# Gated cross-attention and quantised feed-forward, one core: the second stage's rounded rows are turned by transposing transfers instead of TensorE and VectorE

## What is computed

```python
def _quant_per_tensor(x):
    scale = jnp.maximum(jnp.max(jnp.abs(x)), MIN_RANGE) / QP
    return (_ste_round(x / scale), scale)

def _qlinear(x2d, w, b):
    xq, sx = _quant_per_tensor(x2d)
    wq, sw = _quant_per_tensor(w)
    out = jnp.matmul(xq, wq.T) + b[None, :]
    return out * (sw * sx)

h = _qlinear(x.reshape(-1, D), w1, b1)
h = jax.nn.gelu(h, approximate=False)
o = _qlinear(h, w2, b2)

x = x + jnp.tanh(g_xattn[0]) * _L0_xattn_ref(_layernorm(x), ctx, ctx, ...)
x = x + jnp.tanh(g_ffn[0]) * _L0_ffn_ref(_layernorm(x), w1, b1, w2, b2)
```

## Time and profile before

| | us |
|---|---|
| median of 3 runs | 451.65 (450.1 to 454.19) |
| the profiled execution | 451.68 |
| its span, first to last instruction | 449.8 |
| TensorE matmul busy | 411.2 (91%) |
| VectorE busy | 350.6 (78%) |
| ScalarE busy | 275.4 (61%) |
| GpSimd busy | 124.7 (28%) |

### The profile page before, as it was taken

How to read it: one execution, slowest core, us unless ns; L and a number is a source line. 1 busy time by engine, 2 the same in 40 slices (tenths; PEclk the granted TensorE clock), 3 DMA queues, 4 the chain that set the end, 5 groups by cost and what they waited for, 6 DMA issues and landing times.

```text
span 449.8 us, 6567 instructions
## 1 busy us (share of the span) xinstructions
PE 411.2 (91%) x2236; PEld 254.3 (57%) x2236; DVE 350.6 (78%) x666; ACT 275.4 (61%) x478; POOL 124.7 (28%) x169
## 2 busy tenths in 40 slices
PE   6879969999999878868499999999999999999996
PEld 5646858778777567753244444444464444444442
DVE  4887682999996737989998899889759787666762
ACT  2157253897887255838098689869969999560000
POOL 2364671887888140323910000000000000000000
PEclk9997787999999668999699999999999999999999
DMA  6999650293345012124256676400019999962222
GB/s 232 359 366 405 203 195 1 104 313 146 133 146 186 1 38 103 47 94 189 93 240 281 280 305 283 201 1 0 0 34 373 414 425 411 398 212 93 94 95 93
DMA packets 14637, 85.37 MB, mean 190 GB/s; under 512 B 1784, under 2 KB 2048, under 8 KB 5136
## 3 DMA queue, kind: packets, MB, share of 16 engines
q1 hardware_dynamic: 14464, 84.74, 49.6%
q10 hardware_dynamic: 144, 0.26, 0.2%
HBM read 55.64 MB, written 29.36 MB: 189 GB/s over the span
## 4 chain that ended last, share of the span: by engine, by line
PE 78%; DVE 12%; issue 3%; SPq 2%; ACT 2%; DMA 1%; POOL 1%; DVEq 0%; ACTq 0%; POOLq 0%
PE PS L1187 24%; PE PS L1155 23%; PE PS L1070 6%; PE PS L1053 6%; PE PS L1005 6%; PE PS L1051 4%; PE PS L1042 3%; PE PS L1021 3%; DVE ring L853 2%; PE PS L1117 2%; DVE hmax L681 1%; DVE X L717 1%; DMA X<-in_x 1%; SPq L280 1%; PE PS L1013 1%
## 5 line engine op out<-in xcount | busy, mean ns | idle before, releaser
L548 ACT ACTIVATE ring<-PS,bias,sc 128x512 f32<-128x512 f32 x128 | 97.2, 782 | 36.5 <-PE PS L1155 24.6
L1155 PE MATMUL PS<-mid,w1q 128*128 128x512 bf16 x512 | 113.5, 382 | 0.9 <-DVE mid L869 0.9
L1187 PE MATMUL PS<-w2q,w1q 128*128 128x512 bf16 x512 | 110.8, 379 | 1.3 <-DVE w1q L936 0.9
L1187 PEld LDWEIGHTS PS<-w2q,w1q 128*128 128x128 bf16 x512 | 49.9, 98 | 61.9 <-DVE w1q L936 1.4
L1155 PEld LDWEIGHTS PS<-mid,w1q 128*128 128x128 bf16 x512 | 50.1, 99 | 60.6 <-issue 2.7
L882 DVE TENSOR_REDUCE hmax<-ring 128x1 f32<-128x2048 f32 x30 | 68.0, 2280 | 7.5 <-ACT ring L548 7.5
L567 ACT ACTIVATE ring<-ring,sc 128x2048 f32<-128x2048 f32 x31 | 59.7, 1993 | 8.9 <-DMA ring<-spilled_hidden 8.9
L936 DVE TENSOR_SCALAR w1q<-ring 128x2048 bf16<-128x2048 f32 x31 | 37.9, 1224 | 25.0 <-PE PS L1187 21.5
L381 POOL TENSOR_TENSOR X<-X,w2q 128x512 f32 (+1 forms) x30 | 38.1, 1301 | 10.8 <-ACT w2q L494 10.8
L978 PE MATMUL PS<-ident 128*128 128x128 f32 x192 | 27.6, 300 | 10.1 <-POOL ident L364 4.2
L1005 PE MATMUL PS<-ring 128*128 128x129 f32 x256 | 33.8, 296 | 0.4 <-DMA ring<-in_ctx 0.3
(11 more groups left out here) (125 smaller groups left out, 544.3 us busy)
## 6 DMA issues: line engine op xcount, KB each, us to landing
spilled_hidden<-ring SPq DMA_DIRECT2D x20, 1024.0 KB, 3.9
ring<-spilled_hidden SPq DMA_DIRECT2D x20, 1024.0 KB, 9.9
ring<-in_ctx SPq DMA_DIRECT2D x8, 1024.0 KB, 9.5
ring<-in_ctxT SPq DMA_DIRECT2D x8, 1024.0 KB, 4.8
X<-in_x SPq DMA_DIRECT2D x7, 1024.0 KB, 10.2
out<-X SPq DMA_DIRECT2D x7, 1024.0 KB, 11.3
ring<-in_w1T SPq DMA_DIRECT2D x4, 1024.0 KB, 11.6
ring<-in_w2T SPq DMA_DIRECT2D x8, 512.0 KB, 3.6
```

Of the source, the lines that this page charges most:

```text
L548: nc.scalar.activation(ring[:, s * CH + c, (h % CH) * N:(h % CH + 1) * N], PS[:, hidden_bank(s, h), :], ACT.Gelu, scale=S1, bias=bias1[:, ...
L1155: mm = nc.tensor.matmul(PS[:, hidden_bank(s, h), :], w1v[:, k, h * P:(h + 1) * P], xqT[:, s, k, :], start=(k == 0), stop=(k == NH - 1))
L1187: mm = nc.tensor.matmul(PS[:, par * NT + i, :], hq[:, c, k, i * P:(i + 1) * P], w2v[:, kk, :], start=(kk == 0), stop=(kk == KH - 1))
```

## The change

TensorE's 128 transposes in the second stage, VectorE's 16 copies out of PSUM and their two semaphores are gone. In their place SyncE issues 16 transposing transfers for each batch, 128 in all, each from a block of 128 tokens by 128 features in the ring to a block of `xqT`, both in SBUF. Each transfer moves 128 x 128 bf16, 32 KB. For batch g+1 they are issued by `turn_tokens`, which waits on `xq_done`. It stands in SyncE's list behind the store of chunk 0 of group g for g = 0 to 4; for g = 5 and 6 there are no stores. TensorE waits at the start of a group until all 16 transfers of its batch have landed (16 counts each). At the start of the stage four more warming matmuls stand behind each `xq_done` of batch 0.

```diff
-        psX = PS[:, 4:6, :].bitcast(BF16).rearrange("p a (k n) -> p (a k) n", n=N)
+        def integers(s):
+            return ring[:, s * CH + 2, 0:CW // 2].bitcast(BF16).rearrange("p (i k d) -> p i k d", i=NT, k=NH)
...
-            for g in range(SPILLED):
+            def turn_tokens(g):
+                xq = integers(g % SLOTS)
+                wait(sp, h_done, KH * (g - SLOTS + 1))
+                for i in range(NT):
+                    sp.wait_ge(xq_done, 4 * g + i + 1)
+                    for k in range(NH):
+                        sp.dma_start(xqT[:, g % SLOTS, k, i * P:(i + 1) * P], xq[:, i, k, :],
+                                     transpose=True).then_inc(xqT_in[g % SLOTS], 16)
+
+            turn_tokens(0)
+            for g in range(B):
                 for c in range(CH):
-                    sp.wait_ge(gelu_done, KH * g + (c + 1) * KH // CH + len(H_BANK))
-                    sp.dma_start(spill[g * CH + c], ring[:, (g % SLOTS) * CH + c, :]).then_inc(spilled[g % SLOTS], 16)
+                    if g + 1 < B and c == (1 if g < SPILLED else 0):
+                        turn_tokens(g + 1)
+                    if g < SPILLED:
+                        sp.wait_ge(gelu_done, KH * g + (c + 1) * KH // CH + len(H_BANK))
+                        sp.dma_start(spill[g * CH + c], ring[:, (g % SLOTS) * CH + c, :]).then_inc(spilled[g % SLOTS], 16)
...
-            def evacuate(g, s):
-                dve.wait_ge(xT_done, g + 1)
-                for n in range(2):
-                    V.tensor_copy(xqT[:, s, 2 * n:2 * n + 2], psX[:, 2 * n:2 * n + 2]).then_inc(xqT_done, 1)
...
             quantise_x(0, 0, 0)
-            evacuate(0, 0)
...
                 group_max(g, s, 1)
-                if not last:
-                    evacuate(g + 1, (s + 1) % SLOTS)
...
-            transposes(0, 0)
+            for i in range(NT):
+                pe.wait_ge(xq_done, i + 1)
+                keep_warm(4)
...
-                    if h == 3 * KH // 4 and not last:
-                        if g == 0:
-                            pe.wait_ge(w2_step, 6)
-                        transposes(g + 1, (s + 1) % SLOTS)
                     pe.wait_ge(gelu_done, KH * g + h + 1)
                     for k in range(NH):
-                        if h == 0 and k % 2 == 0:
-                            pe.wait_ge(xqT_done, 2 * g + 2 + k // 2)
+                        if h == 0 and k == 0:
+                            pe.wait_ge(xqT_in[s], 16 * NT * NH * (g // SLOTS + 1))
```

More of the change, by code:

```diff
@@ L190, in gated_xattn_ffn @@
         xs_step, xs_pow, scales = (sem(n) for n in ("xs_step", "xs_pow", "scales"))
-        y_done, xq_done, xT_done, xqT_done = (sem(n) for n in ("y_done", "xq_done", "xT_done", "xqT_done"))
+        y_done, xq_done = sem("y_done"), sem("xq_done")
+        xqT_in = [sem(f"xqT_in{s}") for s in range(SLOTS)]
         h_done, gelu_done, hm_done = (sem(n) for n in ("h_done", "gelu_done", "hm_done"))
@@ L344, in _ @@
         def _(pool):
-            for semaphore in [xqT_done, hm_done, product_done] + spilled + hq_used + [a for c in back_in for a in c]:
+            for semaphore in [hm_done, product_done] + spilled + hq_used + [a for c in back_in for a in c]:
                 pool.sem_inc(semaphore, 1)
@@ L1109, in _ @@
             steps(pe, step)
[L1111 to L1118, removed]
             pe.sem_inc(gelu_done, len(H_BANK))
@@ L1142, in group @@
                     if g == 0 and h == KH // 2:
-                        pe.wait_ge(xqT_done, 3)
                         pe.wait_ge(w2_step, 5)
                         across(4, W2MAX).then_inc(w2_all, 1)
-                    if h == 3 * KH // 4 and not last:
-                        if g == 0:
-                            pe.wait_ge(w2_step, 6)
-                        transposes(g + 1, (s + 1) % SLOTS)
                     pe.wait_ge(gelu_done, KH * g + h + 1)
                     for k in range(NH):
-                        if h == 0 and k % 2 == 0:
-                            pe.wait_ge(xqT_done, 2 * g + 2 + k // 2)
+                        if h == 0 and k == 0:
+                            pe.wait_ge(xqT_in[s], 16 * NT * NH * (g // SLOTS + 1))
                         mm = nc.tensor.matmul(PS[:, hidden_bank(s, h), :], w1v[:, k, h * P:(h + 1) * P], xqT[:, s, k, :],
```

## The result

The changed kernel takes 568.65 us (median of 4 runs, 567.85 to 570.65) against 452.92 us before: 1.256 times, with a 95% interval of 1.247 to 1.265. It is 115.7 us slower. The forecast was 510 us, slower. The direction and the place of the wait came out; the size did not, and neither did what makes a transfer dear. 568.65 lies inside the range of 452 to 580, but the loss is twice the 58 us forecast.

A forecast was written before the change was run, and what follows sets the result against it. The prediction took TensorE as pacing the kernel, with transfers too slow to hide under its matmuls. The start, four middle steps and last groups moved the second stage's end from 328.3 to 386.5: 451.7 + 58.2 = 510 us, range 452 to 580.

The forecast's parts named there:

- TensorE paces the steady groups, and a batch's transfers don't fit under 13.8 us of matmuls: Second stage, steady groups: TensorE sets the pace; transfers fit only at 0.33 us spacing or less, 0.44 by the store's path.
- The price t of a transfer, 0.80 us: Time between successive transfers in a batch's 16, the slower of issuing and moving; 0.80 us, likeliest 0.6 to 1.0, chance 0.40.
- The term 105t: Part of the slowdown formula 105t + 7L - 43.3 that grows with the spacing between transfers, t; for t above about 0.5.
- The landing L, 2.5 us: Time from a transfer's issue start to its landing; 2.5 us, upper bound 3.9 us from the 1 MB stores.
- The start, two rounds one behind the other with w2's scale between them: Second stage, groups 0 and 1: two exposed rounds of transfers cost 21 us, group 1 starting at 247.5 instead of 226.3.
- S1: Start of group 1 in the second stage: S0 + 20.3 + 15t + L, forecast 247.5 us (before: 226.3).
- S0: Start of group 0 in the second stage: 198.2 + 15t + L, forecast 212.7 us (before: 201.4).
- The steps of the middle groups, 7.0 + 15t + L: From one group's start to the next, groups 1 to 5: 21.5 us, four times; 7.0 is the wait behind chunk 0's store.
- S6 follows S5 without a gap: Group 6 starts right when group 5's 16.1 us of matmuls end, since batch 6's integers are ready before.
- The restart at half clock, 2.3 us each: TensorE after each long idle time: half clock makes 4.6 us of work cost 2.3 us extra.
- The one at t = 1.3 with 562 us: Rival: transposing transfers dearer than plain packets, perhaps in shorter pieces; +111 us; chance 0.20 for spacing above 1.0 to 1.5.
- Hidden transfers at the kernel before's time: Rival: transfers cost no more than plain issues and hide under matmuls, about 454 us; chance 0.17 for hidden or nearly.

The follow-up runs named there:

- the wide form: Against the changed kernel, each batch turned by 4 transposing transfers of 128 x 512 instead of 16 of 128 x 128: 454.31 us, 1.005 times the kernel before.

## Why the prediction was right in kind and wrong in size

- **TensorE paces the steady groups, and a batch's transfers don't fit under 13.8 us of matmuls**: right. Every group's matmuls wait for a transfer into `mid` and none for VectorE, whose 10 us of copies brought nothing back.
- **The price t of a transfer, 0.80 us**: this is the step that failed. It measured 1.275 us from issue to issue. I took the issue to cost 0.27 to 0.56 us by the plain rows and let the moving of 128 short packets at 0.10 us each set the pace. Both halves were wrong. Moving is cheap: SyncE's queue took 0.430 x 16 x 568.8 = 3913 us for its packets against 3570 before, so 343 us for 20480 more packets, 0.017 us each, six times less than the row I used; 160 packets a transfer are 0.17 us on each of 16 engines. The DMA share of 0.11 while batch 1 was turned gives the same, 0.11 x 16 x 24.8 = 43.6 us for 16 transfers. Issuing is dear: 1.23 us of SyncE, flat from 32 KB to 128 KB. A value near 1.3 could have come only from the upper part of my bounds (up to 1.97 us), and it would have been right for the wrong reason, since that bound is a price of moving too. The term 105t was 84 us in the sum and is 134 us with the measured t.
- **The landing L, 2.5 us**: right, 2.4, with luck. I had taken it from stores to HBM, another kind of transfer, and misread the row: 2.5 us are 256 KB stores, the two of 128 KB took 2.7.
- **The start, two rounds one behind the other with w2's scale between them**: right. With t = 1.275 the formula gives S1 = 218.5 + 38.3 + 5.0 = 261.8, and the first stage of this profile was 2.8 us later than before (the first integers at 201.0 instead of 198.2): 264.6, measured 264.87. That this is so close is two errors that cancel. S0 came at 224.04, 1.4 us late, and from S0 to S1 it took 40.8 us instead of 41.9, mostly since the first 32 matmuls took 8.9 us and not 9.7.
- **The steps of the middle groups, 7.0 + 15t + L**: with the measured t 28.6 us, measured 29.3 to 29.9. The missing us is the first two issues behind a store, for batch 2 2.21 and 1.64 us instead of 1.23. I had said that an issue can be held up by the queue, and did not add it here. Four steps, 4.3 us.
- **S6 follows S5 without a gap**: wrong. It came 26.2 us later, not 16.1. At t = 0.80 SyncE would have been free in time; at 1.275 the transfers of batch 6 queue behind those of batch 5, though its integers were ready at 376.3, 8 us before SyncE came to them. SyncE's timeline has batches 6 and 7 in one piece:

```profile
384.53 44.60 SPq L328 DMA_TRANSPOSE mid<-ring  x32
```

  Most of it is made up at the next step (20.6 us), 2.8 us remain. Together: 105 x 1.275 + 17.5 - 43.3 = 108.1, 0.3 + 4.3 + 2.8 more give 115.5 us, and the last group took 16.9 us instead of 16.1: 116.3. The second stage grew by 119.0 - 2.8 = 116.2 us (its last matmul ended at 447.3 instead of 328.3).
- **The restart at half clock, 2.3 us each**: an upper value. In the first 4.60 us of the eight groups the granted clock was 0.50 to 0.71, with 10 to 15 matmuls against 22 at full clock, so a restart cost 1.3 to 2.3 us. The one after 24.93 us of waiting:

```profile
264.90:269.50 4.60, 4.60 (x12) 1.66 (x13) 0.00 (x0) 1.55 (x2) 0.00 (x0) 0.54 1.02 420
```

- **The rivals.** The one at t = 1.3 with 562 us was the nearest, and its reason, that turning makes shorter pieces to move, was not the one: the plain transfers took 144 packets each and 327 us of queue time for all 128 (0.498 x 16 x 489.1, less 3570), the turned ones 160 and 343 us. Hidden transfers at the kernel before's time are what the wide form gives: the rival's conclusion holds, for a quarter of the instructions. The Trainium skill's 1309 ns for a transposing transfer ("VectorE: DVE Perf Modes", section "The three transpose paths") gave +112 us as the spacing, and this case's trace agrees with it as that: 1232 ns for an issue and 1275 ns between two. I had set it aside because its 390 ns for TensorE are not the spacing there (0.056 us). The Trainium skill's rule that transposing transfers are as fast as regular ones ("Advanced Engine Details and Errata", section "X-Bar Transpose (TRN2)") agrees with the moving (0.17 us a transfer turned, 0.16 plain) and not with the issuing: 0.60 us plain, 1.23 turned.

## What to carry to other kernels

A transfer has two prices, the issuing engine's time and the moving, and the issue price of one kind (a store) says little of another's (a turn within SBUF). Before many small ones replace work on a compute engine, multiply their count by an issue measured on one of their own kind, and set it against the time that should hide them. If they are too dear, put more into each before moving them about: four feature blocks in one instruction brought back 114 of 116 us, the better place in the queue brought 7 to 9. Where a saving is small (0.89 us a group here), keep the pieces that nothing can hide, such as the first batches of a stage, on the engine that does them at once.

## What was not expected of the hardware

- A transposing transfer within SBUF costs SyncE 1.23 us to issue at 128 x 128, 1.27 at 128 x 512, and 1.8 to 2.3 at 128 x 2048 (bf16); landing takes 2.4, 2.5 and 4.6 us.
- A plain transfer of 128 rows of 256 bytes within SBUF costs 0.60 us to issue (0.47 at least) and lands in 1.9 us, while a 1 MB store to HBM costs 0.32 us to issue.
- These issues are dear with idle DMA engines too: 1.10 us for the first one of batch 1, and 11% of DMA time while 16 are issued in a row.
- Behind 4 MB of stores just issued, the first three transposing transfers took 2.2 to 2.8 us each to issue (in the kernel with the transfers ahead of the store).
